# Running the last layers of three narrow batch tiles once, side by side in 512 columns

## The reference

```python
def reference(dense_ctx, ids, tbl_0, ..., W_top1, b_top1, W_top2, b_top2, W_top3, L0_rec_kernels):
    e = jnp.stack([tbl_0[ids[:, 0]], ...], axis=1)            # (2048, 32, 64)
    II, JJ = np.triu_indices(32, k=1)                          # 496 pairs
    z = jnp.sum(e, axis=-1)                                    # (2048, 32)
    outer = jnp.einsum('bpd,pde,bpe->bp', e[:, II, :], kernels, e[:, JJ, :])
    h = jnp.concatenate([z, outer, dense_ctx], axis=1)         # (2048, 544)
    h = jnp.maximum(h @ W_top1 + b_top1, 0.0)                  # 512 columns
    h = jnp.maximum(h @ W_top2 + b_top2, 0.0)                  # 256 columns
    return h @ W_top3                                          # 1 column
```

## Time and profile before

| | us |
|---|---|
| Median of 3 runs (lowest, highest) | 874.92 (874.81, 875.81) |
| Profiled execution, its own time | 875.68 |
| Its span in the profile | 873.9 |
| TensorE busy, matmuls | 840.1 (96%) |
| VectorE busy | 623.2 (71%) |
| GpSimd busy | 494.5 (57%) |
| ScalarE busy | 151.9 (17%) |

### The profile page before, as it was taken

One profiled execution on the slowest core, in us unless ns is written; L12 is line 12 of the kernel. 1 busy time (PEld: TensorE's weight loads), 2 busy tenths in 40 slices (PEclk: granted clock), 3 DMA queues, 4 the chain that ended last, 5 costly groups with the idle time before them and its releaser, 6 DMA issues.

```text
span 873.9 us, 15786 instructions
## 1 busy us (share of the span) xinstructions
PE 840.1 (96%) x6584; PEld 404.9 (46%) x6584; DVE 623.2 (71%) x706; ACT 151.9 (17%) x273; POOL 494.5 (57%) x550
## 2 busy tenths in 40 slices
PE   1899999999999999999999999999999999999997
PEld 1788888766655333333333333333333333333332
DVE  0677577688866788888855488888845588888840
ACT  1212312212210220020210320020211312020001
POOL 7875777777777777777776477667723430000000
DMA  9511111111111111111111011111100000000000
GB/s 325 187 28 23 28 31 29 28 28 31 28 28 27 28 27 27 30 28 27 28 26 25 17 25 26 23 27 27 26 12 13 16 14 1 1 1 1 1 1 1
DMA packets 24209, 28.32 MB, mean 32 GB/s; under 512 B 13254, under 2 KB 13385, under 8 KB 24012
## 3 DMA queue, kind: packets, MB, share of 16 engines
q0 software_dynamic: 16384, 16.81, 10.7%
q1 hardware_dynamic: 7744, 10.49, 3.6%
q10 hardware_dynamic: 12, 0.01, 0.0%
HBM read 27.27 MB, written 0.01 MB: 31 GB/s over the span
## 4 chain that ended last, share of the span: by engine, by line
PE 92%; DVE 3%; POOL 2%; DMA 1%; issue 1%; ACT 1%; DVEq 0%; ACTq 0%
PE y L615 50%; PE acc L632 26%; PE y L662 7%; PE y L598 4%; PE y L678 3%; DVE prod L563 3%; POOL rows L369 2%; PE y L667 1%; DMA rows<-tbl,ids_sb 1%; PE y L688 1%; POOL spare L368 1%; DMA ids_sb<-ids 0%; ACT h_in L445 0%; PE y L644 0%; ACT h L482 0%
## 5 line engine op out<-in xcount | busy, mean ns | idle before, releaser
L563 DVE TENSOR_TENSOR prod<-y,xt 128x1024 f32<-128x1024 f32 (+2 forms) x600 | 582.4, 1033 | 199.4 <-PE y L615 198.3
L369 POOL DMA_INDIRECT rows<-tbl,ids_sb x512 | 483.4, 944 | 214.0 <-issue 111.2
L615 PE MATMUL y<-xt,kw 64*128 64x512 f32 (+2 forms) x2976 | 476.9, 463 | 4.3 <-DVE prod L563 3.2
L615 PEld LDWEIGHTS y<-xt,kw 64*128 64x128 f32 x2976 | 244.0, 190 | 217.0 <-issue 199.4
L632 PE MATMUL acc<-prod,ones_strip 128*32 128x512 f32 (+2 forms) x2976 | 239.4, 454 | 0.3 <-DVE prod L563 0.3
L632 PEld LDWEIGHTS acc<-prod,ones_strip 128*32 128x32 f32 x2976 | 79.4, 109 | 142.4 <-issue 68.1
L414 ACT COPY xt<-y 128x1024 f32<-128x1024 f32 (+3 forms) x56 | 36.2, 646 | 300.8 <-PE y L598 300.7
L662 PE MATMUL y<-h_in,w_sb 128*128 128x512 f32 (+2 forms) x192 | 58.4, 457 | 3.1 <-ACT h_in L445 2.6
L598 PE MATMUL y<-ident,rows 128*128 128x128 f32 x256 | 41.4, 289 | 20.5 <-DMA rows<-tbl,ids_sb 20.4
L535 DVE TENSOR_REDUCE z_rows<-rows 128x8 f32<-128x512 f32 (+2 forms) x96 | 44.6, 500 | 17.2 <-DMA rows<-tbl,ids_sb 17.2
L445 ACT COPY h_in<-acc 128x512 f32<-128x512 f32 (+2 forms) x24 | 10.6, 443 | 240.4 <-PE acc L632 240.4
(11 more groups left out here) (22 smaller groups left out, 55.1 us busy)
## 6 DMA issues: line engine op xcount, KB each, us to landing
rows<-tbl,ids_sb POOLq DMA_INDIRECT x512
kw<-pair_k SPq DMA_DIRECT2D x14, 512.0 KB, 11.9
w_sb<-w SPq DMA_DIRECT2D x1, 1024.0 KB, 12.2
w_sb<-w SPq DMA_DIRECT2D x1, 512.0 KB, 13.6
kw<-pair_k SPq DMA_DIRECT2D x1, 384.0 KB, 18.3
ids_sb<-ids SPq DMA_DIRECT2D x1, 256.0 KB, 2.7
kw<-pair_k SPq DMA_DIRECT2D x1, 256.0 KB, 4.2
w1z_sb<-w1z SPq DMA_DIRECT2D x1, 256.0 KB, 12.3
```

Source lines behind the costliest of these rows:

```text
L369: pool.indirect_dma_start(out=rows[:, s, c, h, :], out_offset=None, in_=tables[f], in_offset=bass.IndirectOffsetOnAxis(ap=ids_sb[:, b, f:f ...
L563: nc.vector.tensor_tensor(prod_part(t, d, n), y_part(t, d, n), x, ALU.mult).then_inc(y_read, n)
L615: last = nc.tensor.matmul(y[:, h, :], kw[part, d, :], xt[part, slot_of(t, units[h][0] // 2), 0:w], start=True, stop=True)
```

## The change

`MLP_TILES` groups the tiles into four of 512 columns: tiles 0, 1 and 2 together, and 3, 4 and 5 alone. `mlp_of(t)` gives a tile's group and its columns in it. ScalarE writes a tile's `h_in` and `z_in` into its own columns, and the last layers run once for a group, placed behind its last tile: for tiles 0 to 2 in tile 3, where tile 2's own layers stood. The bodies of `mlp2`, `mlp3`, `read_mlp2` and `read_mlp3` change like those shown, from `0:w` to all 512 columns.

```diff
+MLP_TILES = [[0, 1, 2], [3], [4], [5]]
+def mlp_of(t):
+    m = next(m for m, tiles in enumerate(MLP_TILES) if t in tiles)
+    first = sum(WIDTHS[b] for b in MLP_TILES[m] if b < t)
+    return m, slice(first, first + WIDTHS[t])
...
-    for d, what in zip(MLP_STEPS, (("mlp1", t - 1, 0), ("mlp1", t - 1, 1), ("mlp2", t - 1, 0), ("mlp3", t - 1, 0))):
-        work[groups(t)[1] + d].append(what)
+    m, _ = mlp_of(t - 1)
+    if t - 1 == MLP_TILES[m][-1]:
+        for d, what in zip(MLP_STEPS, (("mlp1", m, 0), ("mlp1", m, 1), ("mlp2", m, 0), ("mlp3", m, 0))):
+            work[groups(t)[1] + d].append(what)
...
-                if t > 0:
-
-                    act.wait_ge(y_full, y_use("mlp1", t - 1, 1) + 1)
+                m, cols = mlp_of(t)
+                if m > 0:
+
+                    act.wait_ge(y_full, y_use("mlp1", m - 1, 1) + 1)
                 w = WIDTHS[t]
-                nc.scalar.copy(h_in[:, c, 0:w], accs[(CHUNKS * t + c) % 2][:, 0:w]).then_inc(acc_read, 1)
+                nc.scalar.copy(h_in[:, c, cols], accs[(CHUNKS * t + c) % 2][:, 0:w]).then_inc(acc_read, 1)
...
-                nc.scalar.copy(z_in[:, 0:w], y_banks[u % Y_SLOTS][:, 0, 0:w]).then_inc(act_read, 1)
+                nc.scalar.copy(z_in[:, cols], y_banks[u % Y_SLOTS][:, 0, 0:w]).then_inc(act_read, 1)
...
-                    last = nc.scalar.activation(h1[:, j, 0:w], y_banks[u % Y_SLOTS][:, h, 0:w], ACT.Relu,
+                    last = nc.scalar.activation(h1[:, j, :], y_banks[u % Y_SLOTS][:, h, :], ACT.Relu,
                                                 bias=b1_sb[:, j:j + 1])
...
-                act.dma_start(out[0:1, P * first_block(t):P * first_block(t) + w], h1[0:1, 0, 0:w]
+                act.dma_start(out[0:1, TILE * m:TILE * m + TILE], h1[0:1, 0, :]
                               ).then_inc(out_stored, 16)
...
-                    pe.wait_ge(acc_read, CHUNKS * (t + 1))
-
-                    pe.wait_ge(act_read, act_uses_through(y_use("fields", t, 0)))
-                w = WIDTHS[t]
-                y = take_y(y_use("mlp1", t, pair))
+                    pe.wait_ge(acc_read, CHUNKS * (MLP_TILES[m][-1] + 1))
+
+                    pe.wait_ge(act_read, act_uses_through(y_use("fields", MLP_TILES[m][-1], 0)))
+                y = take_y(y_use("mlp1", m, pair))
...
-                        nc.tensor.matmul(y[:, h, 0:w], w1_sb[:, c, j * P:(j + 1) * P], h_in[:, c, 0:w],
+                        nc.tensor.matmul(y[:, h, :], w1_sb[:, c, j * P:(j + 1) * P], h_in[:, c, :],
                                          start=c == 0, stop=False)
```

More of the change, by code:

```diff
@@ L124, in first_block @@
     return sum(WIDTHS[:t]) // P
+MLP_TILES = [[0, 1, 2], [3], [4], [5]]
+assert all(sum(WIDTHS[t] for t in tiles) == TILE for tiles in MLP_TILES)
+def mlp_of(t):
+    m = next(m for m, tiles in enumerate(MLP_TILES) if t in tiles)
+    first = sum(WIDTHS[b] for b in MLP_TILES[m] if b < t)
+    return m, slice(first, first + WIDTHS[t])
 AHEAD = 6
@@ L182, in plan @@
         order.append(("sum", t, len(groups(t)) - 2))
-        order += [("mlp1", t, 0), ("mlp1", t, 1), ("mlp2", t, 0), ("mlp3", t, 0)]
+        m, _ = mlp_of(t)
+        order += [("mlp1", m, 0), ("mlp1", m, 1), ("mlp2", m, 0), ("mlp3", m, 0)]
     return order
@@ L449, in read_fields, with read_mlp1 @@
                 w = WIDTHS[t]
+                _, cols = mlp_of(t)
                 act.wait_ge(y_full, u + 1)
-                nc.scalar.copy(z_in[:, 0:w], y_banks[u % Y_SLOTS][:, 0, 0:w]).then_inc(act_read, 1)
-            def read_mlp1(t, pair):
-                u = y_use("mlp1", t, pair)
-                w = WIDTHS[t]
-                if t == 0 and pair == 0:
+                nc.scalar.copy(z_in[:, cols], y_banks[u % Y_SLOTS][:, 0, 0:w]).then_inc(act_read, 1)
+            def read_mlp1(m, pair):
+                u = y_use("mlp1", m, pair)
+                if m == 0 and pair == 0:
                     act.wait_ge(small_loaded, 48)
                 elif pair == 0:
-                    act.wait_ge(y_full, y_use("mlp2", t - 1, 0) + 1)
-                    act.wait_ge(out_stored, 16 * t)
+                    act.wait_ge(y_full, y_use("mlp2", m - 1, 0) + 1)
+                    act.wait_ge(out_stored, 16 * m)
                 act.wait_ge(y_full, u + 1)
@@ L468, in read_mlp1, with read_mlp2, read_mlp3 @@
                     j = 2 * pair + h
-                    last = nc.scalar.activation(h1[:, j, 0:w], y_banks[u % Y_SLOTS][:, h, 0:w], ACT.Relu,
+                    last = nc.scalar.activation(h1[:, j, :], y_banks[u % Y_SLOTS][:, h, :], ACT.Relu,
                                                 bias=b1_sb[:, j:j + 1])
                 last.then_inc(act_read, 1)
[L473 to L478, removed]
+            def read_mlp2(m):
+                u = y_use("mlp2", m, 0)
+                if m > 0:
+                    act.wait_ge(y_full, y_use("mlp3", m - 1, 0) + 1)
                 act.wait_ge(y_full, u + 1)
                 for j in range(J2):
-                    last = nc.scalar.activation(h2[:, j, 0:w], y_banks[u % Y_SLOTS][:, j, 0:w], ACT.Relu,
+                    last = nc.scalar.activation(h2[:, j, :], y_banks[u % Y_SLOTS][:, j, :], ACT.Relu,
                                                 bias=b2_sb[:, j:j + 1])
                 last.then_inc(act_read, 1)
-            def read_mlp3(t):
-                u = y_use("mlp3", t, 0)
-                w = WIDTHS[t]
+            def read_mlp3(m):
+                u = y_use("mlp3", m, 0)
                 act.wait_ge(y_full, u + 1)
-                nc.scalar.copy(h1[0:1, 0, 0:w], y_banks[u % Y_SLOTS][0:1, 0, 0:w]).then_inc(act_read, 1)
+                nc.scalar.copy(h1[0:1, 0, :], y_banks[u % Y_SLOTS][0:1, 0, :]).then_inc(act_read, 1)
                 act.wait_ge(act_read, act_uses_through(u))
-                act.dma_start(out[0:1, P * first_block(t):P * first_block(t) + w], h1[0:1, 0, 0:w]
+                act.dma_start(out[0:1, TILE * m:TILE * m + TILE], h1[0:1, 0, :]
                               ).then_inc(out_stored, 16)
@@ L513, in _ @@
                     read_mlp3(t)
-            act.wait_ge(out_stored, 16 * TILES)
+            act.wait_ge(out_stored, 16 * len(MLP_TILES))
         @block.vector
@@ L646, in transpose_fields, with mlp1 @@
                 last.then_inc(y_full, 1)
-            def mlp1(t, pair):
+            def mlp1(m, pair):
                 if pair == 0:
-                    if t == 0:
+                    if m == 0:
                         pe.wait_ge(weights_loaded, 48)
-                    pe.wait_ge(acc_read, CHUNKS * (t + 1))
-                    pe.wait_ge(act_read, act_uses_through(y_use("fields", t, 0)))
-                w = WIDTHS[t]
-                y = take_y(y_use("mlp1", t, pair))
+                    pe.wait_ge(acc_read, CHUNKS * (MLP_TILES[m][-1] + 1))
+                    pe.wait_ge(act_read, act_uses_through(y_use("fields", MLP_TILES[m][-1], 0)))
+                y = take_y(y_use("mlp1", m, pair))
                 for h in range(2):
@@ L666, in mlp1, with mlp2, mlp3 @@
                     j = 2 * pair + h
-                    last = nc.tensor.matmul(y[:, h, 0:w], w1z_sb[part, j * P:(j + 1) * P], z_in[part, 0:w],
+                    last = nc.tensor.matmul(y[:, h, :], w1z_sb[part, j * P:(j + 1) * P], z_in[part, :],
                                             start=False, stop=True)
                 last.then_inc(y_full, 1)
[L671 to L675, removed]
+            def mlp2(m):
+                pe.wait_ge(act_read, act_uses_through(y_use("mlp1", m, 1)))
+                y = take_y(y_use("mlp2", m, 0))
                 for j in range(J2):
                     for c in range(J1):
-                        last = nc.tensor.matmul(y[:, j, 0:w], w2_sb[:, c, j * P:(j + 1) * P], h1[:, c, 0:w],
+                        last = nc.tensor.matmul(y[:, j, :], w2_sb[:, c, j * P:(j + 1) * P], h1[:, c, :],
                                                 start=c == 0, stop=c == J1 - 1)
                 last.then_inc(y_full, 1)
[L682 to L686, removed]
+            def mlp3(m):
+                pe.wait_ge(act_read, act_uses_through(y_use("mlp2", m, 0)))
+                y = take_y(y_use("mlp3", m, 0))
                 for c in range(J2):
-                    last = nc.tensor.matmul(y[0:1, 0, 0:w], w3_sb[:, c:c + 1], h2[:, c, 0:w],
+                    last = nc.tensor.matmul(y[0:1, 0, :], w3_sb[:, c:c + 1], h2[:, c, :],
                                             start=c == 0, stop=c == J2 - 1)
```

## The result

The changed kernel takes 889.56 us (median of 4 runs, 888.74 to 890.52), the one before 875.37 us: a ratio of 1.0162, 95% interval 1.0145 to 1.018. It is 14.2 us slower. The profiled execution took 889.0 us for a span of 887.2.

A forecast was written before the change was run, and what follows sets the result against it. TensorE was taken as the bound, level with GpSimd's gathers at 236.05 us. Span 873.9 + 12.1 (work behind that point) + 1.9 (clock) = 887.9, plus 1.78 around it, less 0.76 to the median: 888.9 us, range 886.2 to 891.2.

The forecast's parts named there:

- The chain of gathers: GpSimd's 128 gathers from 75.07 to 234.58 us, one every 1.25 us, claimed to run without being held by anyone.
- couple 5 of tile 3: Transposes TensorE starts at 236.05 us, in tile 2's second half, exactly level with the gathers; claimed to land then as before.
- a moved start of the chain: Sign of being wrong: the gathers' start, at 75.08 us before, or their period moves.
- The 14.2 us taken out in front of it: Blocks of tiles 0 and 1, run within tiles 1 and 2, leave TensorE before 236.05 us.
- two waits of 7.3 and 7.6 us: TensorE's waits for gathered rows at couples 3 and 5 of tile 3, claimed to absorb its 14.2 us lead.
- 12.1 us more behind it: After 236.05 us, the new 512-column block's 25.5 us replaces tile 2's 13.4, and nothing absorbs the difference.
- 1.9 us for the clock: Slow matmuls and transpose after the second wait, as TensorE restarts from idle; size taken from the kernel's start.
- Nothing behind couple 5 waits for ScalarE's wide reads or a buffer: After 236.05 us, wide reads, output DMA and the h_in wait are claimed to be as in tiles 4 and 5.
- What the change saves is 2.1 us: Whole kernel: TensorE has 2.1 us less work, with 14.2 and 12.8 us leaving and 24.9 coming in.
- rival 2: Gathers aren't the bound: tile 3's couples land 14.2 us sooner, the whole saving stays, 872.4 us; chance 0.05.
- The further 0.4 us: The wait ahead of tile 0's block, which the faster rival counted as saved besides the 2.1 us.
- The sum of 888.9: Forecast median for the whole changed kernel: 888.9 us, 1.6% slower; the forecast case has chance 0.60.

The follow-up runs named there:

- run 1: Kernel before, with only one of two fields of each couple gathered for tile 2 (32 gathers fewer): 873.62 us, ratio 0.9985.
- run 2: Changed kernel, with only one of two fields of each couple gathered for tile 2: 871.51 us, ratio 0.9962.
- run 5: Changed kernel, with tile 1's first transposes and tile 0's fields' transpose 8 or 4 steps earlier, so gathers start sooner: 886.4 us, ratio 1.0131.
- 6: Kernel before, with tile 1's first transposes and tile 0's fields' transpose 8 or 4 steps earlier: 873.62 us, ratio 0.9987.
- run 7: Changed kernel, with transposes of tile 3's couples 2 to 5 later and the new block's second pair moved forward: 875.0 us, ratio 0.9999.
- run 4: Kernel before, with the three narrow blocks of tiles 0 to 2 moved into tile 3 but not joined: 890.11 us, ratio 1.0173.
- run 8: Changed kernel with both the earlier transposes for the gathers' start and the later requests for tile 3's couples: 872.44 us, ratio 0.9966.
- run 3: Kernel before, with only tiles 0 and 1 joined, in tile 2; tile 2's own block stays in tile 3: 876.03 us, ratio 1.0013.

## Why the prediction was right

- *The chain of gathers is a second full engine, and TensorE is level with it at couple 5 of tile 3.* Right. 128 gathers at 1.25 us again, and couple 5 at 234.93, 1.1 us sooner and not 14. Runs 1 and 2 show it by taking the gathers away, 5 and 6 by moving the chain, 7 by moving TensorE's requests. The prediction named a moved start of the chain as a sign of being wrong, and the start did move, by 1.41 us; but that came from the pace of TensorE's first 34 us, which varies between executions whatever the edit.
- *The 14.2 us taken out in front of it are lost in two waits of 7.3 and 7.6 us.* They are 7.55 and 5.29. The second is shorter because the low clock behind the first slowed TensorE by 2.2 us on the way (3.70 − 2.00, and 1.12 − 0.65 for the transposes). That the second wait covers this slow stretch was forecast, but it wasn't taken off the 7.6. It makes no difference to the end: 7.55 + 5.29 + 2.2 = 15.0, and 7.3 + 7.6 = 14.9 were forecast.
- *12.1 us more behind it.* 12.0 by the rows of the blocks.
- *1.9 us for the clock.* 2.4, now with the granted clock as evidence. How near it came is in part luck. The stretch behind couple 5 cost 2.0 us in run 4 (3.53 − 2.00, and 1.12 − 0.65) and 1.5 in run 5 (3.03 − 2.00, and 1.11 − 0.65), so 2.4 is one draw of several. And that the kernel's start, from which the 1.9 was taken, ran at the lower clock is inferred: its ratio of pace, 3.79 / 2.06 = 1.84, is nearly that behind the first wait, 3.70 / 2.00 = 1.85, but the trace lists 1.00 for it.
- *Nothing behind couple 5 waits for ScalarE's wide reads or a buffer.* Right: the waits for `h_in` ahead of the blocks of tiles 3 to 5 are 2.1 us in both kernels, the wait ahead of the new block is 0.54 us in place of 0.49, and behind couple 5 none is for a buffer or for rows. In run 2, with the same block, it is the same.
- *What the change saves is 2.1 us.* Right: 2.1 between runs 1 and 2 in medians, 2.2 in spans. The further 0.4 us that rival 2 and run 2's expectation added for the wait ahead of tile 0's block don't show in this difference.
- *The gathers aren't the bound, 872.4 us*, the rival on the other side: it is what happens once the gathers are given room. Its condition wasn't met. Run 8's 872.4 is the same figure only in part for the same reason, since 1.1 us of its gain come from the early transposes and not from joining.

The sum of 888.9 is 0.7 us under the median of 889.56. Most of this is the kernel before, whose median is 875.37 with the fourth run beside it in place of the 874.92 that the sum started from; the forecast difference was 14.0 us and the measured one is 14.2.

## What to carry to other kernels

An engine with a constant pause between its instructions can be full though its busy share is far from it, as GpSimd was here at 76% with a pause of 0.30 us: count its instructions between two moments and look whether any pause differs from the others. In run 1, where it had room, its longest wait was 8.6 us. Where a queue of loads is level with the bounding engine, find the last place at which they meet; here work taken away ahead of it was lost (run 3) and work put behind it was paid in full (run 4), so moving work across it cost its whole length though there was less of it. The remedy is to let the requests come later (put the moved work ahead of them) or to start the loads sooner, and here each alone was not enough to make the change pay.

## What the runs showed of the hardware

The granted clock fell to its lower level behind waits of 7.55 and 5.29 us, and also behind one of only 1.74 us (run 7). Behind a wait of 2.42 us in the profiled execution of run 3 the matmuls kept their pace, 2.00 us for 16, and behind the 0.71 us of the kernel before too. So a short wait may or may not cost as much again in clock. The Trainium skill has the gate fall after an idle stretch and rise after sustained work (TensorE: Matmul & The Clock Gate, Part 1: The HAM clock gate). The two long waits agree with that; a fall behind 1.74 us isn't what the Trainium skill leads one to expect there, and the measurement stands. The same part of the Trainium skill calls the moment of the rise variable from run to run; the first 34 us of this kernel agree with it, in so far as they are the clock's doing: the same 32 matmuls took 3.79 us in some executions and 2.06 in others.
